# A recurrent-attention kernel: two temporaries of the scan move from SBUF to PSUM, and the first steps of the attention stage are put in another order

## The reference, cut to what matters

```python
def step(h, xt):
    xr_t, xz_t, xn_t = xt
    r = jax.nn.sigmoid(xr_t + h @ w_hr.T + b_hr)
    z = jax.nn.sigmoid(xz_t + h @ w_hz.T + b_hz)
    n = jnp.tanh(xn_t + r * (h @ w_hn.T + b_hn))
    h_new = (1.0 - z) * n + z * h
    return (h_new, h_new)
```

```python
k = (1 - smear) * k + smear * k_prev
pos = jnp.cumsum(jax.nn.sigmoid(y).transpose(0, 2, 1), axis=-1)
relpos = pos[..., :, None] - pos[..., None, :]
mask = causal - relpos
scores = jnp.einsum('bhid,bhjd->bhij', q / s, k / s) / np.sqrt(D_HEAD) + mask
attn = jax.nn.softmax(scores, axis=-1)
```

## Time and profile before

| | |
|---|---|
| Median of three runs | 1612.38 us (1610.09 to 1614.88) |
| The profiled execution's own time | 1611.58 us |
| Its span in the profile | 1609.9 us, 67304 instructions |
| Busy: PE / DVE / ACT / POOL | 1368.7 / 1171.9 / 712.7 / 435.9 us |
| Mean granted TensorE clock | 0.963 of full speed |
| Scan | `n_` runs 512 times, first at 25.7 us, last at 1010.3 us |
| Attention's first instruction on DVE / first exponent on ACT | 1045.9 / 1101.0 us |

### The profile page before, as it was taken

One profiled execution on the slowest core, in us unless ns is written; L12 is line 12 of the kernel. 1 busy time (PEld: TensorE's weight loads), 2 busy tenths in 40 slices (PEclk: granted clock), 3 DMA queues, 4 the chain that ended last, 5 costly groups with the idle time before them and its releaser, 6 DMA issues. The chain is left out here.

```text
span 1609.9 us, 67304 instructions
## 1 busy us (share of the span) xinstructions
PE 1368.7 (85%) x27835; PEld 988.2 (61%) x27850; DVE 1171.9 (73%) x6266; ACT 712.7 (44%) x2475; POOL 435.9 (27%) x821
## 2 busy tenths in 40 slices
PE   5888888888888888888888888468999999999886
PEld 4777777777777777777777777324445455444443
DVE  5767777777777777777777777477687787777485
ACT  3333323333323333232333332135777777777764
POOL 2101111111111111111111111355255545622364
PEclk7999999999999999999999999677999999999998
DMA  5100000000000000000000000049447635751001
GB/s 119 32 4 5 5 5 7 5 5 7 5 5 7 5 5 7 5 6 5 7 5 5 7 5 6 8 104 158 73 79 124 76 74 98 104 76 27 1 14 40
DMA packets 68951, 53.81 MB, mean 33 GB/s; under 512 B 12686, under 2 KB 68390, under 8 KB 68646
## 3 DMA queue, kind: packets, MB, share of 16 engines
q1 hardware_dynamic: 66470, 49.32, 18.4%
q10 hardware_dynamic: 2176, 0.20, 0.1%
HBM read 31.84 MB, written 15.47 MB: 29 GB/s over the span
## 5 line engine op out<-in xcount | busy, mean ns | idle before, releaser
L739 PEld LDWEIGHTS PS<-GB,W 128*128 128x128 f16 x18432 | 505.1, 96 | 263.5 <-DVE GB L1058 263.3
L739 PE MATMUL PS<-GB,W 128*128 128x32 f16 x18432 | 556.0, 177 | 129.6 <-DVE GB L1058 124.8
L951 ACT ACTIVATE tr<-PS 128x16 f32<-128x16 f32 x512 | 93.8, 183 | 502.7 <-PE PS L739 502.7
L2411 DVE CUSTOM_DVE_ANT_0 masked<-PS,maskD 128x256 bf16<-128x256 f32 (+3 forms) x512 | 231.4, 484 | 84.7 <-PE PS L1860 82.7
L2144 ACT ACTIVATE PT<-PS 128x512 f32<-128x512 f32 (+1 forms) x352 | 193.1, 566 | 98.5 <-PE PS L1881 94.2
L806 PE MATMUL PS<-W 128*128 128x256 f16 x1248 | 220.3, 272 | 0.0
L1044 DVE SCALAR_TENSOR_TENSOR u_<-tr,PS 128x16 f32<-128x16 f32 x512 | 87.6, 171 | 116.5 <-PE PS L739 102.7
L953 ACT ACTIVATE tz<-PS 128x16 f32<-128x16 f32 x512 | 93.8, 183 | 175.4 <-PE PS L739 175.4
L692 POOL TENSOR_TENSOR rt<-mv,eps 128x1 f32<-128x1 f32 x96 | 18.2, 190 | 548.0 <-DVE mv L1069 548.0
L1860 PE MATMUL PS<-KS,QS 99*128 99x256 bf16 (+3 forms) x512 | 136.1, 318 | 19.9 <-DVE MX L2411 12.4
L1051 DVE SCALAR_TENSOR_TENSOR zg<-tz,HR 128x16 f32<-128x16 f32 x512 | 90.3, 176 | 70.8 <-ACT tz L953 1.1
(11 more groups left out here) (397 smaller groups left out, 2410.4 us busy)
## 6 DMA issues: line engine op xcount, KB each, us to landing
QS<-q_parts SPq DMA_DIRECT2D x90, 128.0 KB, 11.2
KS<-k_parts SPq DMA_DIRECT2D x90, 128.0 KB, 14.1
q_parts<-PQ SPq DMA_DIRECT2D x16, 384.0 KB, 11.5
k_parts<-PK SPq DMA_DIRECT2D x16, 384.0 KB, 3.3
X<-XM SPq DMA_DIRECT2D x32, 64.0 KB
out_dram<-X SPq DMA_DIRECT2D x8, 256.0 KB, 2.3
XM<-in_L_attn_x_dram SPq DMA_DIRECT2D x16, 80.0 KB
s_hh<-in_L_attn_w_hh_dram SPq DMA_DIRECT2D x1, 768.0 KB, 5.3
```

Of the source, the lines that this page charges most:

```text
L739: return pe.matmul(bank[:, p, end - wide:end], W[:, kc, w:w + P], GBF[:, state - wide:state], start=False, stop=True, skip_group_check=True)
L951: act.activation(as_states(tr), now(pR), ACT.Tanh, scale=gate_scale).then_inc(hn_tr.sem, 1)
L2411: last = dve.tensor_tensor_reduce(out=masked[:, k % 2, at], in0=p_x[:, k % 2, at], in1=maskD[:, S - w:], scale=-1.0, scalar=3.0e38, op0=AL ...
```

## The change

There are three parts.

1. In the scan, `v_` and `n_` are no longer SBUF tiles but columns 128 to 143 and 144 to 159 of the bank pair pR, in the half `p` of the step. DVE writes `v_` into PSUM, ACT reads it there and writes `n_` into PSUM, DVE reads it there. The number and order of instructions in a step stay.
2. In attention's `start`, the two groups' maxima follow each other: the second group's items stand between `max_parts` and `rows_of_maxima` of the first. `positions(1)` moves on PE to the end of `first_sequences`; what PE, ACT and DVE did in `second_sequence` moves between the value projections (after i = 32). A new `third_sequence`, after both groups, holds POOL's split of sequence 1's keys and scales, and DVE's moments of sequence 2.
3. The extra key rows of sequence 0 are written to DRAM and read back by ACT's queue, not SP's.

```diff
-            v_ = sb(ctx, "v_", [P, NSTEP])
-            n_ = sb(ctx, "n_", [P, NSTEP])
+            SPARE = HC * BLOCK
+            v_ = [PS[:, i, SPARE + 0 * NSTEP:SPARE + 1 * NSTEP] for i in range(2)]
+            n_ = [PS[:, i, SPARE + 1 * NSTEP:SPARE + 2 * NSTEP] for i in range(2)]
...
-                    act.activation(n_[:, :], v_[:, :], ACT.Tanh, scale=n_scale).then_inc(n_ready.sem, 1)
+                    act.activation(n_[p], v_[p], ACT.Tanh, scale=n_scale).then_inc(n_ready.sem, 1)
...
-                    dve.tensor_tensor(by_chunk(v_[:, :]), by_chunk(u_[:, :]), xn, ALU.add).then_inc(v_ready.sem, 1)
+                    dve.tensor_tensor(by_chunk(v_[p]), by_chunk(u_[:, :]), xn, ALU.add).then_inc(v_ready.sem, 1)
...
-                    dve.scalar_tensor_tensor(zn[:, :], tz[:, :], 1.0, n_[:, :], ALU.subtract, ALU.mult).then_inc(zn_ready.sem, 1)
+                    dve.scalar_tensor_tensor(zn[:, :], tz[:, :], 1.0, n_[p], ALU.subtract, ALU.mult).then_inc(zn_ready.sem, 1)
...
                     for i in range(SLOTS):
                         project_v(0, 0, i, None)
+                        if i == 32:
+                            second_sequence()
                     for j in range(NT):
                         for n in range(len(ITEMS[j])):
                             maxima(0, 0, 0, j, n)
-                    for k in range(NI):
-                        max_parts(0, 0, 0, k)
-                        rows_of_maxima(0, 0, 0, k, None)
-                    second_sequence()
                     for j in range(NT):
                         for n in range(len(ITEMS[j])):
+                            max_parts(0, 0, 0, FIRST[j] + n)
+                            rows_of_maxima(0, 0, 0, FIRST[j] + n, None)
                             maxima(0, 0, 1, j, n)
+                    third_sequence()
...
                     out(1, parts_q, q_out, qd, PQ)
-                    sp.wait_ge(kaT.sem, kaT.value(sp, 0))
-                    sp.dma_start(ad[0], KAT[:, :]).then_inc(a_out.sem, 16)
-                    sp.wait_ge(a_out.sem, a_out.value(sp, 0))
-                    sp.dma_start(KS[96:KF, 0, :, :], ad[0].rearrange("(h r) n -> r h n", r=6)).then_inc(first_in[0].sem, 16)
                     back(QS, qd, q_order, h1, first_in[1])
...
                 def second_sequence():
+                    pass
+
+                def third_sequence():
                     split(1, 2)
                     split(1, 3)
                     scales(2)
...
                     product(1, 3, 4)
+                    positions(1)
 
                 def second_sequence():
-                    positions(1)
                     pe.wait_ge(qk.sem, qk.value(pe, 1))
                     extra_rows(1, 4)
...
                     extra_rows(0, 6)
+                    act.wait_ge(kaT.sem, kaT.value(act, 0))
+                    act.dma_start(ad[0], KAT[:, :]).then_inc(a_out.sem, 16)
                     smear_gate(1)
                     queries(1, 1, 5)
                     keys(1, 1, 4)
+                    act.wait_ge(a_out.sem, a_out.value(act, 0))
+                    act.dma_start(KS[96:KF, 0, :, :], ad[0].rearrange("(h r) n -> r h n", r=6)).then_inc(first_in[0].sem, 16)
...
                 def second_sequence():
                     smear(1, 1)
                     extra_rows(1)
+
+                def third_sequence():
                     moments_of(2)
```

More of the change, by code:

```diff
@@ L948, in steps @@
                     now = lambda bank: bank[:, p, 0:HC * BLOCK].rearrange("p (c u b) -> p c u b", c=HC, b=B)[:, :, LEAD // B + k, :]
-                    as_states = lambda x: x[:, :].rearrange("p (c b) -> p c b", c=HC)
+                    as_states = lambda x: x.rearrange("p (c b) -> p c b", c=HC)
                     act.wait_ge(r_ps.sem, n)
-                    act.activation(as_states(tr), now(pR), ACT.Tanh, scale=gate_scale).then_inc(hn_tr.sem, 1)
+                    act.activation(as_states(tr[:, :]), now(pR), ACT.Tanh, scale=gate_scale).then_inc(hn_tr.sem, 1)
                     act.wait_ge(z_ps.sem, n)
-                    act.activation(as_states(tz), now(pZ), ACT.Tanh, scale=gate_scale).then_inc(tz_ready.sem, 1)
+                    act.activation(as_states(tz[:, :]), now(pZ), ACT.Tanh, scale=gate_scale).then_inc(tz_ready.sem, 1)
                     act.wait_ge(v_ready.sem, n)
-                    act.activation(n_[:, :], v_[:, :], ACT.Tanh, scale=n_scale).then_inc(n_ready.sem, 1)
+                    act.activation(n_[p], v_[p], ACT.Tanh, scale=n_scale).then_inc(n_ready.sem, 1)
                 def inputs(j, s):
@@ L1462, in build, with sequences @@
             block = ctx.enter_context(nc.Block())
-            def sequences(eng, item, max_parts, values_late, heads_out, rows_of_maxima, output, project_v, project_qk, maxima, first_sequences, second_sequence, beside_last):
+            def sequences(eng, item, max_parts, values_late, heads_out, rows_of_maxima, output, project_v, project_qk, maxima, first_sequences, second_sequence, third_sequence, beside_last):
                 def start():
@@ L1708, in max_parts @@
                         pool.tensor_tensor(part(5), MR[:, :, :], part(4), ALU.subtract).then_inc(qa.sem, 2)
-                sequences(pool, nothing, max_parts, nothing, nothing, nothing, output, nothing, project_qk, nothing, first_sequences, second_sequence, beside_last)
+                sequences(pool, nothing, max_parts, nothing, nothing, nothing, output, nothing, project_qk, nothing, first_sequences, second_sequence, third_sequence, beside_last)
                 last = (B - 1, 1)
@@ L2017, in beside_last @@
                         turn_in(0)
-                sequences(pe, item, nothing, values_late, heads_out, rows_of_maxima, output, project_v, project_qk, maxima, first_sequences, second_sequence, beside_last)
+                sequences(pe, item, nothing, values_late, heads_out, rows_of_maxima, output, project_v, project_qk, maxima, first_sequences, second_sequence, third_sequence, beside_last)
                 last = (B - 1, 1)
@@ L2203, in beside_last @@
                         high(0)
-                sequences(act, item, nothing, values_late, nothing, rows_of_maxima, output, project_v, project_qk, nothing, first_sequences, second_sequence, beside_last)
+                sequences(act, item, nothing, values_late, nothing, rows_of_maxima, output, project_v, project_qk, nothing, first_sequences, second_sequence, third_sequence, beside_last)
                 last = (B - 1, 1)
@@ L2519, in beside_last @@
                         f_low(0)
-                sequences(dve, item, nothing, nothing, heads_out, nothing, output, project_v, project_qk, maxima, first_sequences, second_sequence, beside_last)
+                sequences(dve, item, nothing, nothing, heads_out, nothing, output, project_v, project_qk, maxima, first_sequences, second_sequence, third_sequence, beside_last)
                 last = (B - 1, 1)
```

## The result

The changed kernel takes 1592.36 us (median of four runs, 1591.01 to 1592.88), the kernel before in the same comparison 1613.63 us (1610.09 to 1615.58): a ratio of 0.9869, 95% interval 0.985 to 0.9889, so 21.3 us faster. Forecast were 1589 and 1573 to 1604. The profiled execution took 1592.88 us, its span is 1591.2 against 1609.9, and its instructions are as many, 67304.

The account below looks back on a forecast made before the run. The prediction took the scan's slackless chain, 1.927 us a step and 985 of 1609.9 us, as the main bound, with waits at attention's start. 1611.58 - 19.5 - 3.7 = 1588.4, so 1589 for the median; range 1573 to 1604.

Parts of the forecast that it names:

- attention's 3.7 us: Start of attention: with the new order the first `XN` begins at 1097.4 instead of 1101.13, -3.7 us.
- ACT reads PSUM, -33 ns: Scan: ACT reading `v_` in PSUM shortens `n_` from 216 to 183 ns, as `tr` takes, -33 ns a step.
- The writes, taken as nothing: Scan: DVE writing `v_` and ACT writing `n_` in PSUM, each -33 to +33 ns, together taken as nothing.
- Rival A: Scan: the writes to PSUM help too, up to 57 ns a step, -29 us; 1579 in all; chance 0.26.
- its ceiling: Scan: `zg`'s start stays, so `zn` comes at most 0.05 us earlier; with its own 5 ns, 57 ns a step.
- DVE reads PSUM, -5 ns: Scan: DVE reading `n_` in PSUM shortens `zn` from 176 to 171 ns; its start may shift, -5 to +5.
- The scan's sum: Scan: 33 from ACT's read and 5 from DVE's make 38 ns a step, times 512 = -19.5 us.
- Part 3: Attention's start: read-back on ACT's queue starts several us earlier, first maxima stop waiting for it; SP's later DMAs 3.1 earlier.
- I let some overlap and start DVE's first maxima 0.5 us later than now: Start of attention: 4.4 us of inserted work against DVE's idle 3.58 delays the first maxima by 0.5, to 1078.6.
- Beyond that the order of `body` is the same, so the lead stays: Attention behind the first `XN`: the 3.7 us gained there last to the end of the kernel.
- Rival D: Attention: inserted work is not covered and third group's stacks are late, no gain: 1592; a fifth of the forecast's 0.50.
- POOL's RR, DVE waits for it some 2 us: Start of attention: POOL's scales come at 1097.4, DVE is ready at 1095.6 and waits some 2 us before `XN`.

Follow-up runs that it names:

- v_only: The kernel before with only `v_` moved into PSUM, `n_` staying an SBUF tile: 1600.2 us, ratio 0.9936.
- n_only: The kernel before with only `n_` moved into PSUM, `v_` staying an SBUF tile: 1596.88 us, ratio 0.9912.
- rows_by_sp: The changed kernel with the extra key rows of sequence 0 written and read back by SP again: 1589.79 us, ratio 0.9877.
- attention_only: The changed kernel with `v_` and `n_` back in SBUF, so only the attention order and ACT's queue are changed: 1613.22 us, ratio 1.0008.
- scales_first: The changed kernel with POOL's scales of sequence 2 ahead of its split of sequence 1's keys, and DVE's moments ahead of them: 1589.5 us, ratio 0.9876.
- attention_late: The kernel before in the scan, with the attention order of rows_late: 1605.26 us against 1610.62, ratio 0.997.
- rows_late: scales_first with PE's turn and ACT's copy of sequence 1's extra rows behind both groups' maxima: 1585.65 us, ratio 0.9841.
- late_pool: rows_late with POOL's sum into XM, once in 16 scan steps, held back until the next step's state is there: 1581.94 us, ratio 0.982.
- fill_after: The changed kernel with an unread 256-column matmul on PE ahead of each score item of the first two groups: 1594.42 us, ratio 0.99.
- best: late_pool with the unread 256-column matmul of fill_after ahead of each score item of the first two groups: 1584.93 us, ratio 0.9843.

## Why the prediction was right, and where it was not

**The time** was 1592.4 for 1589, and inside the likeliest case's 1583 to 1597. In part that is luck: it hides one step that failed (attention's 3.7 us) and, in the scan's sum, errors that cancelled.

**ACT reads PSUM, -33 ns:** right (v_only, 183). The row of another instruction of the same engine, function and shape was the whole evidence, and held to the nanosecond.

**The writes, taken as nothing:** each end was real. ACT's write is worth -29 alone and -15 beside the read; DVE's costs +8. The premise, that one is nearer where the other is farther, has the right signs but not equal sizes. The Trainium skill, ScalarE: Activation LUTs, section Step-by-step, says that ScalarE writes PSUM faster and VectorE is the one nearer to SBUF; n_only's 187 against 216 and v_only's 179 against 171 agree. Rival A had the mechanism, and its ceiling was not reached: `zn` still starts 0.10 behind `zg`. (The ceiling was added up wrongly, too: 50 and 5 ns make 55, not 57.)

**DVE reads PSUM, -5 ns:** -5 on `zn` (n_only), and the gap to `GB` is unchanged. The Trainium skill's figures for DVE, 60 ns on SBUF and 125 on PSUM (Perfetto Trace Analysis, Optimizing Scalar/DVE Operations), are not borne out by these rows: 171 with `n_` in PSUM, 176 with it in SBUF. The page calls its figures engine-busy times and says that the latency in a profile is about twice as long; the prediction's +12 us took them as they are. Doubled they would be further off still.

**The scan's sum:** 38 ns forecast, 39 measured, and the agreement is luck: with the terms that were taken as nothing a usual step has -47, and some 8 came back, POOL's sum in one step of 16 (4 in the mean) and a rest that is untraced. The forecast had taken `zg`'s start as fixed and did not look at what else lengthens `zg`.

**Part 3:** right that the first maxima cease to wait for `k_extra`, wrong on why: the read-back was forecast several us earlier on ACT's queue and came 1.7 us earlier, and the maxima come late enough for SP's queue as well (rows_by_sp). ACT's queue has neither a price nor a worth that these runs can tell.

**Part 2, the step that failed:** "I let some overlap and start DVE's first maxima 0.5 us later than now". It was 2.4 (attention_only) to 3.9 us later. The 4.4 us of inserted work were set against DVE's idle 3.58, but they do not stand in one row on DVE: PE waits for DVE (2.89), then DVE, through ACT, for PE (3.22 and 1.28). PE's two pairs of projections behind that wait took 1.94 and 1.69 us at a granted clock of 0.52 and 0.59; in the kernel before, at a clock of 1.00, the same two took 1.12 and 1.02:

```profile
1070.90 1.12 PE L1847 MATMUL PS<-winT,XT 128*128 128x512 f32 x2 [0.59 <-DVE SP L2399]
1071.86 0.38 PE L1848 MATMUL PS<-bv,ones_w 128*128 128x512 bf16 x1
1072.08 1.02 PE L1847 MATMUL PS<-winT,XT 128*128 128x512 f32 x2
```

**"Beyond that the order of `body` is the same, so the lead stays":** also wrong. Of the forecast -3.7, the first exponent had all (-3.7, in attention_only -5.2), `XN` -0.8 to -2.3, and the positions of sequence 2 nothing (0.0 in attention_only, +1.5 in the changed kernel). Of the 5.1 us that were given back, 2.6 are PE's waits for DVE ahead of the transposes of `XN`, 1.7 of them behind the wait for RR that the prediction had itself put there, and 2.5 are the same matmuls at the lower clock, which it had not looked at. Rival D, 1592, had this outcome, but its second cause, late stacks of the third group, is not what did it: PE's waits there are for DVE's maxima, not for a DMA.

**POOL's RR, DVE waits for it some 2 us:** it waited 1.66, behind the same POOL order. That without it the gain would be 5.5 was wrong: scales_first, which takes it away, ends 0.8 us nearer to its last `zn` than the kernel before.

What stays open: why TensorE's clock comes back 8 to 12 us sooner after the first exponent with the extra rows late (attention_late, rows_late, late_pool). PE's busy share around the first exponent doesn't tell the kernels apart (6.64 of 7 us in scales_first at 0.50, 6.33 in late_pool at 0.85), and with a filler that kept it up before (fill_after) it fell 4 us behind the exponent and came back no sooner.

## What to carry to other kernels

In a chain of short instructions look for the same engine, function and shape with its operand elsewhere, and take its duration; but price two accesses of one instruction together, since here -33 and -29 made -48. Work that is inserted into a wait is covered only if it needs no other engine in between; count the hand-overs, not the sum. And where PE's stretch follows a rearranged start, read the granted clock there as well: a lead of 4 us was worth nothing until the clock came back with it. Moving 0.6 us of matmuls and a copy out of the way, with the moments and scales in earlier places, was worth 6. late_pool has the lowest median of these kernels, 1581.94 us; its interval overlaps with those of rows_late and best.

## What the runs showed of the hardware that was not expected

ACT on PSUM: 216 ns (SBUF to SBUF), 183 (reads PSUM), 187 (writes it), 168 (both), for 16 columns. DVE's write to PSUM costs 8 ns, its read saves 5. A DVE instruction on two SBUF operands takes 260 ns instead of 175 while POOL adds 128x128 numbers in SBUF. And TensorE's clock can stay at its lower level for 14 us while PE is busy 7.00 of 7 us in the second half of them (changed kernel), so a busy PE is not yet a fast one.
